# A two-layer gated cross-attention and FFN kernel: the first FFN's weights turned and split inside the attention's last slots, and the butterfly's path products moved to the FFN's first stage

## What is computed

```python
x = x + tanh(g_xattn[0]) * L0_attention(layernorm(x), ctx)     # 16 heads of 16
# first FFN, quantised
x1 = act_qdq(layernorm(x))              # one scale for the whole tensor
up = act_qdq(x1 @ lpbq_dequant(w_up).T)     # w_*: 4 bit, blocks of 32, 768 x 256
gate = act_qdq(x1 @ lpbq_dequant(w_gate).T)
sig = fixed_qdq_u16(sigmoid(gate))
gate = act_qdq(gate * sig)
x = x + tanh(g_ffn[0]) * (act_qdq(gate * up) @ lpbq_dequant(w_down).T)
x = x + tanh(g_xattn[1]) * L1_attention(layernorm(x), ctx)     # 8 heads of 64
# second FFN: W_exp, 10 butterfly stages of width 1024, gelu, 10 stages, W_con
x = x + tanh(g_ffn[1]) * L1_ffn(layernorm(x))
```

## Time and profile before

| | |
|---|---|
| median of three runs | 1106.67 us |
| the profiled execution: its own time, its span | 1109.04, 1106.8 us |
| mean granted TensorE clock | 0.917 |
| busy in the span: PE, DVE, ACT, POOL | 937.6, 788.3, 616.5, 247.8 us |
| setup and slots of the first attention | 0 to 302 us |
| first FFN: setup block, to the first gate product | 302 to 323 us |
| gate products; up products; code stage; down products | 323 to 399; to 487; to 552; to about 650 us |

### The profile page before, as it was taken

How to read it: one execution, slowest core, us unless ns; L and a number is a source line. 1 busy time by engine, 2 the same in 40 slices (tenths; PEclk the granted TensorE clock), 3 DMA queues, 4 the chain that set the end, 5 groups by cost and what they waited for, 6 DMA issues and landing times. The chain is left out here.

```text
span 1106.8 us, 20169 instructions
## 1 busy us (share of the span) xinstructions
PE 937.6 (85%) x6641; PEld 830.2 (75%) x6641; DVE 788.3 (71%) x1585; ACT 616.5 (56%) x1067; POOL 247.8 (22%) x436
## 2 busy tenths in 40 slices
PE   6589999999569998824088994999999998999998
PEld 5467787877358876613088993999999986999888
DVE  5358888874339989879979833677777777766671
ACT  4147777764367779968747633556656653322230
POOL 4223333320139200013004202111111104111210
PEclk9779999997769999966579996999999998999999
DMA  6755555552042237778422367755656620000001
GB/s 189 219 132 143 143 142 142 145 172 81 6 159 115 114 119 235 254 254 288 147 79 73 138 205 169 171 122 121 124 124 125 125 65 1 20 20 26 31 19 39
DMA packets 101076, 138.31 MB, mean 125 GB/s; under 512 B 42758, under 2 KB 76550, under 8 KB 98582
## 3 DMA queue, kind: packets, MB, share of 16 engines
q1 hardware_dynamic: 100102, 135.23, 43.3%
q10 hardware_dynamic: 608, 1.18, 0.5%
q0 software_dynamic: 304, 1.10, 0.3%
HBM read 71.04 MB, written 47.13 MB: 107 GB/s over the span
## 5 line engine op out<-in xcount | busy, mean ns | idle before, releaser
L2645 ACT ACTIVATE f_h<-bank,f_b 128x512 f32<-128x512 f32 x64 | 43.4, 691 | 112.1 <-PE bank L43 64.3
L665 DVE TENSOR_REDUCE a_maxima<-bank 128x4 f32<-128x308 f32 x128 | 60.4, 472 | 43.8 <-PE bank L738 42.5
L41 PE MATMUL bank<-f_xt_hi,f_w_all 128*128 128x512 f32 x192 | 77.5, 404 | 11.9 <-DMA f_xt_lo<-x_spill 9.9
L599 ACT ACTIVATE a_prob<-bank 77x512 f32<-77x512 f32 x128 | 72.2, 588 | 19.5 <-PE bank L763 19.2
L42 PE MATMUL bank<-f_xt_lo,f_w_all 128*128 128x512 f32 x192 | 75.8, 395 | 0.0
L43 PE MATMUL bank<-f_xt_hi,f_w_all 128*128 128x512 f32 x192 | 75.7, 394 | 0.0
L760 PE MATMUL bank<-a_stack,a_kb 96*77 96x256 f32 x256 | 72.5, 306 | 1.1 <-ACT a_prob L599 0.6
L43 PE MATMUL bank<-f_w_hi,f_h_lo 128*128 128x256 f32 x256 | 72.2, 282 | 0.0
L42 PE MATMUL bank<-f_w_lo,f_h_hi 128*128 128x256 f32 x256 | 72.2, 282 | 0.0
L41 PE MATMUL bank<-f_w_hi,f_h_hi 128*128 128x256 f32 x256 | 72.0, 281 | 0.0
L763 PE MATMUL bank<-a_mt,a_pick 128*77 128x256 f32 x256 | 67.9, 288 | 0.0
(11 more groups left out here) (322 smaller groups left out, 3173.8 us busy)
## 6 DMA issues: line engine op xcount, KB each, us to landing
u_spill<-f_ubuf SPq DMA_DIRECT2D x48, 256.0 KB, 2.7
f_w_all<-u_spill SPq DMA_DIRECT2D x24, 512.0 KB, 4.4
a_stack<-a_queries SPq DMA_DIRECT2D x16, 512.0 KB, 5.2
a_q_max<-a_q_hi SPq DMA_DIRECT2D x30, 256.0 KB, 4.9
a_kb<-a_key_spill SPq DMA_DIRECT2D x96, 77.0 KB, 2.5
xres<-in_x SPq DMA_DIRECT2D x16, 256.0 KB, 4.6
a_queries<-a_q_hi SPq DMA_DIRECT2D x16, 256.0 KB, 3.8
a_queries<-a_q_lo SPq DMA_DIRECT2D x16, 256.0 KB, 4.1
```

The lines of the kernel that those rows point to most:

```text
L41: nc.tensor.matmul(out, w_hi, m_hi, start=start, stop=False)
L599: act.activation(prob[0:S, n % 4, :, :].rearrange("p a b -> p (a b)"), (S0, S1)[n % 2][0:S, :], ACT.Exp, scale=SCALE).then_inc(probs, 1)
L665: dve.tensor_reduce(maxima[:, t, 4 * k:4 * k + 4], MX[:, 0:4 * SE].rearrange("p (h s) -> p h s", s=SE)[:, :, 0:S], AX.X, ALU.max).then_inc ...
L2645: act.activation(h[:, n % 2, :], hbank[n % 4][:, :], ACT.Gelu, bias=b1[:, n:n + 1]).then_inc(h_ready, 1)
```

## The change

- The split weights of the first FFN (`w_all`, `d_hi`, `d_lo`) are allocated before the attention (`FirstFfn`). While the attention's setup runs, they hold the context's and the projections' split parts; the weights to be quantised (`fw`) lie where the keys were, so their loads wait for the keys' store.
- The store to `w_quantised`, the load of it and the whole setup block of the FFN go away. In slots 13, 14 and 15 three steps are added, `turn0` to `turn2`: four transposes on TensorE into bank T0, a 128x512 copy on ScalarE and a 128x512 subtraction on VectorE each, nine in all. The scale of x and the gate's tanh move to the start of the FFN's first block. There VectorE encodes and casts half of the first group.
- The butterfly's low paths are read in one DMA (128x4064) at the head of that block, ahead of the gate's value `tg`, into the room of the `hid` tile that the last two groups fill later. GpSimd forms the path products ahead of the top stages; SyncE stores them (`blocks_spill`) and they are read back in the code stage, behind chunk 5; `y` is read behind chunk 7 and `z` behind chunk 9.
- The three early reads of `u_spill` stand behind all 48 stores.
- In the code stage ScalarE codes all 24 chunks of up. The five units of `y` and the bias stand behind chunks 19 to 23. The four units of `z` move to the next stage: TensorE makes them behind the maximum's spread, ahead of the down products, and ScalarE copies two of them out before each of its first two splits.

```diff
         wo_lo = sb("wo_lo", [P, C, D], F32R)
-        k_hi = sb("k_hi", [P, B, C, SE], F32R)
-        k_lo = sb("k_lo", [P, B, C, SE], F32R)
+        keys_then_fw = sb("keys_then_fw", [P, 2 * B * C * SE])
+        k_hi, k_lo = (keys_then_fw[:, n * B * C * SE:(n + 1) * B * C * SE].bitcast(F32R).rearrange(
+            "p (b c s) -> p b c s", c=C, s=SE) for n in range(2))
...
+        PE_SLOT = "s0 s1 xt turn0 mx0 s2 t3 s3 mx1 s4 q0 turn1 mx2 p1 s5 mx3 p3 s6 mx4 s7 at0 mx5 t0 q1 turn2 mx6 p5 t1 mx7 pr0 pr1 mt t2 p7".split()
+        ACT_SLOT = "s0 s1 xt turn0 s2 st2 s3 p1 s4 turn1 s5 p3 s6 at0 q1 turn2 s7 xn p5 mt p7".split()
+        DVE_SLOT = "mx0 xs turn0 mx1 norm mx2 w0 w1 w2 turn1 mx3 ln mx4 w3 mx5 as mx6 am w4 turn2 mx7 qs pu st1 w5".split()
...
-        SP_SLOT = "xl qw vb k0 qr k1 fw".split()
+        SP_SLOT = "xl qw vb k0 qr k1".split()
...
         def _(sp):
+            sp.wait_ge(kb_stored, 32)
             for n, w in enumerate(("w_gate", "w_up")):
...
-                elif what == "fw":
-                    sp.wait_ge(fw_done, FW_PIECES)
-                    for n in range(3):
-                        sp.dma_start(ffn["quantised"][:, n, :], fw[:, n * FW:(n + 1) * FW]).then_inc(fw_sent, 16)
-
             slots(sp, SP_SLOT, step, SP_SLOT)
-            sp.wait_ge(fw_sent, 48)
...
+                elif what[:4] == "turn":
+                    n = (b - FW_FROM) * 3 + int(what[4])
+                    act.wait_ge(fw_turned, n + 1)
+                    act.activation(FW_TURNS[n][1][0], T0[:, :], ACT.Copy).then_inc(fw_rounded, 1)
...
+                elif what[:4] == "turn":
+                    n = (b - FW_FROM) * 3 + int(what[4])
+                    dve.wait_ge(fw_rounded, n + 1)
+                    dve.tensor_tensor(FW_TURNS[n][1][1], T0[:, :], FW_TURNS[n][1][0].bitcast(F32),
+                                      ALU.subtract).then_inc(fw_split, 1)
...
+                elif what[:4] == "turn":
+                    n = (b - FW_FROM) * 3 + int(what[4])
+                    if n == 0:
+                        pe.wait_ge(fw_done, FW_PIECES)
+                        pe.wait_ge(q_split, B)
+                    else:
+                        pe.wait_ge(fw_split, n)
+                    for k, (tile, col) in enumerate(FW_TURNS[n][0]):
+                        at = tile * D + col
+                        last = pe.transpose(T0[:, k * P:(k + 1) * P], fw[:, at:at + P], ident[:])
+                    last.then_inc(fw_turned, 1)
...
-            @block.sync
-            def _(sp):
-                for n in range(3):
-                    sp.dma_start(wval[:, n * FT:(n + 1) * FT, :].rearrange("p f d -> p (f d)"),
-                                 weights[:, n, :]).then_inc(w_in[n], 16)
-                sp.dma_start(tg[:], gate).then_inc(g_in, 16)
...
-            @block.tensor
-            def _(pe):
...
-                    last.then_inc(turned, 1)
...
                 dve.tensor_scalar(x_step[:], env["rstd_all"][:], codes[:, SX:SX + 1], None, ALU.mult).then_inc(x_scaled, 1)
                 dve.tensor_scalar(x_start[:], env["nmr_all"][:], codes[:, SX:SX + 1], None, ALU.mult).then_inc(x_scaled, 1)
+                dve.wait_ge(x_scaled, 2)
+                for t in range(GTT // 2, GTT):
+                    last = dve.tensor_scalar(xcode[:, t, :], xres[:, t, :], x_step[:, t:t + 1], x_start[:, t:t + 1],
+                                             ALU.mult, ALU.add)
+                last.then_inc(x_half, 1)
+                dve.wait_ge(x_half, 1)
+                dve.tensor_copy(xn[:, GTT // 2:GTT, :], xcode[:, GTT // 2:GTT, :]).then_inc(x_half, 1)
...
+                act.wait_ge(g_in, 16)
+                act.activation(tg[:], tg[:], ACT.Tanh)
                 act.wait_ge(x_scaled, 2)
-                encode(0)
-                cast(0)
+                encode(0, GTT // 2)
+                cast(0, GTT // 2)
+                act.wait_ge(x_half, 2)
                 encode(1)
...
+                        if g == PATH_GROUP and f == 0:
+                            act.wait_ge(blocks_stored, 16)
...
+                pool.wait_ge(paths_in, 16)
+                for s in range(1, LOW):
+                    for net in range(2):
...
+                sp.dma_start(paths, bf["low_paths"]).then_inc(paths_in, 16)
+                sp.dma_start(tg[:], gate).then_inc(g_in, 16)
                 for g in range(G - 2):
+                    if g == PATH_GROUP - 2:
+                        for net in range(2):
+                            sp.wait_ge(composed[net], LOW - 1)
+                        sp.dma_start(bf["blocks_dram"], paths[:, 2 * LOWEST:2 * LOWEST + 2 * HT * P]).then_inc(
+                            blocks_stored, 16)
...
-                    if k == PREFETCH_AT and f == FT - 1:
-
-                        sp.wait_ge(prods, GATES)
-                        for i in range(NR):
-                            written = ORDER.index(i * CW // (2 * FT * T)) * FT + FT
-                            for n in range(NU):
-                                sp.wait_ge(u_sent[n], 16 * ((written + NU - 1 - n) // NU))
-                            fetch_up(sp, i)
+                for i in range(NR):
+                    written = ORDER.index(i * CW // (2 * FT * T)) * FT + FT
+                    for n in range(NU):
+                        sp.wait_ge(u_sent[n], 16 * ((written + NU - 1 - n) // NU))
+                    fetch_up(sp, i)
...
-            DVE_CODES = [1, 9, 17]
...
+            UNITS_FROM = NCH - HT // 2 - 1
+            DVE_CODES = []
...
-                sp.dma_start(blocks[:].rearrange("p n t m -> p (n t m)"), bf["low_last"]).then_inc(last_in, 16)
                 for n in range(len(u_sent)):
                     sp.wait_ge(u_sent[n], 16 * GATES // len(u_sent))
-                sp.dma_start(early[:], bf["low_early"]).then_inc(early_in, 16)
                 for i in range(NR, NCH):
                     u_in(i)
                     if i == 5:
+                        sp.dma_start(blocks[:].rearrange("p n t m -> p (n t m)"), bf["blocks_dram"]).then_inc(blocks_in, 16)
+                    if i == 7:
                         sp.dma_start(y[:], bf["w_exp_t"].rearrange("(t p) d -> p t d", p=P)).then_inc(y_in, 16)
-                    if i == 7:
+                    if i == 9:
                         sp.dma_start(z[:], bf["w2_dram"]).then_inc(z_in, 16)
...
-                pe.wait_ge(composed[0], LOW - 1)
+                pe.wait_ge(blocks_in, 16)
                 pe.wait_ge(y_in, 16)
-                for n in range(HT // 2 + 1):
-                    unit(n)
-                pe.wait_ge(composed[1], LOW - 1)
-                pe.wait_ge(z_in, 16)
-                for n in range(HT // 2 + 1, len(UNITS)):
-                    unit(n)
+                pe.wait_ge(multiplied, UNITS_FROM - 1)
+                for n in range(HT // 2):
+                    for t in range(2 * n, 2 * n + 2):
+                        last = pe.matmul(unit_bank[n][:, (t - 2 * n) * D:(t - 2 * n + 1) * D], blocks[:, 0, t, :],
+                                         y[:, t, 0:D], start=True, stop=True)
+                    last.then_inc(unit_prod, 1)
...
-                for b in range(4):
-                    hi(b)
+                for n in range(HT // 2):
+                    act.wait_ge(unit_prod, n + 1)
+                    act.activation(z[:, 2 * n:2 * n + 2, :], kv_banks[n][:, :].rearrange("p (t d) -> p t d", d=D),
+                                   ACT.Copy).then_inc(unit_out, 1)
+                    if n % 2:
+                        hi(n // 2)
+                hi(2)
+                hi(3)
...
+                pe.wait_ge(z_in, 16)
+                for n in range(HT // 2):
+                    if n == HT // 2 - 1:
+                        pe.wait_ge(e_scale, 1)
+                    for t in range(2 * n, 2 * n + 2):
+                        last = pe.matmul(kv_banks[n][:, (t - 2 * n) * D:(t - 2 * n + 1) * D], blocks[:, 1, t, :],
+                                         z[:, t, :], start=True, stop=True)
+                    last.then_inc(unit_prod, 1)
```

234 lines of the change are left out of this document (102 added, 132 removed).

## The result

The changed kernel takes **1096.96 us**, the median of 5 runs (1093.79 to 1100.34); the kernel before takes 1106.67 us (5 runs, 1104.99 to 1108.11). The ratio is 0.9914, with a 95% interval of 0.9888 to 0.9940. Forecast were 1090.8 us and a range of 1084 to 1100. The profiled execution took 1098.77 us, with a span of 1097.0 us and a mean granted clock of 0.919.

The account below looks back on a forecast made before the run. The prediction took the kernel as a chain of stages, where gains at five hand-overs reach the end unless the clock takes them back. Terms -3.8 - 5.6 - 1.3 - 4.2 - 1.0 = -15.9 off 1106.67 gave 1090.8 us, range 1084 to 1100.

Parts of the forecast that it names:

- Term 1: Attention slots 13 to 15: added turns cost 0.6, 0.6 and 1.2 us, slot 14 at full clock saves 6.2; -3.8 us.
- Rival 1: Slot 14 of the attention: the clock falls all the same, slots 13 to 15 become +2.0 us, total 1096.6 us; chance 0.28.
- Term 2: Start of the first FFN: weight reload and transposes gone, `tg` waits behind the paths; first gate product -5.6 us, bounds -4.3 to -12.8.
- Term 3: End of the up products: three early reads no longer stand ahead of the last six stores; -1.3 us.
- Term 4: Code stage: path products moved out, VectorE codes no chunk and sets the pace; 58.1 us against 62.3, -4.2 us.
- bound by the reads: Code stage: 1 MB reads behind chunks 5, 7 and 9 set the pace, its saving falls to nothing, 1095 us; chance 0.08.
- Term 5: Start of the down products: first split 1.4 us later, twenty-nine products at full clock save 2.7; together -1.0 us.

## Why the prediction was right, and for which reasons it was not

The direction and the range were right: 9.7 us were gained and 15.9 forecast. That the time fell inside the range was in part luck: one term had the wrong sign, one most of its size missing, and a gain that no term had looked at made up for much of both.

**Term 1 failed at the step "If it stays at full, slot 14 is like slot 13, with 19.35 - 13.12 = 6.2 us less. I take that."** The fall of the clock in slot 14 was read from one execution and charged to every one. In its second profile the kernel before, with a wait of 1.34 us in the same place, ran slot 14 in 13.84 us, and the three profiles with other addresses had 13.52, 13.57 and 13.62. Against those 38.03 us for the three slots the change has 38.9: where the clock doesn't fall, term 1 is +0.9, not -3.8. Against the mean of the two profiles, 40.9, it is -2.0; how often the timed runs of the kernel before had the fall, no run shows. The wait for keys did go, as forecast, but not by the reason given: it stays away with the store put back too. The added turns were priced about right: slot 13 is 0.60 longer than in the first profile (0.6 forecast), slot 15 is 0.39 longer (1.2 forecast). The prediction's own sentence that its durations come from an execution 2.4 us above the median should have been a warning: the fall alone made it some 5.5 us longer (19.35 against 13.84).

**Rival 1**, that the clock falls all the same, gives 1096.6, and the time came out at 1097.0; but not by its mechanism. The clock stayed full through slots 13 to 15 with the transposes in them, in all nine profiles of kernels that have the turns. The rule of the Trainium skill behind it (TensorE: Matmul & The Clock Gate, Part 4: PE-mode transpose: a transpose doesn't count as busy in the same way) is neither borne out nor refuted by that, since four transposes stand among score products; against it still speak. That 1096.6 is so near is luck.

**Term 2 held, at its nearer bound**: -4.6 measured from the scale to the first product in the first profiles and -3.9 in the second ones (18.66 to 14.75), -4.3 on the mean; -5.6 was forecast, with a bound of -4.3. The mechanism, `tg` behind the paths, was right to the row. What was off in the first profile is the landing: 9.9 us instead of 9.3, from an issue 0.4 us later than I had it. With `tg` first, the price of the wait is 8.0 us; I had given 7.2 for it.

**Term 3**: the idle time of 1.65 and 1.31 us at the last up products is gone, as forecast. But gate and up products together took 167.2 us before and 166.9 after, on the mean of two. After the change the first gate products run at 1.2 GHz for 6.2 and 3.7 us, before it for 2.9 and 5.4, and the stage is longer the longer that lasts; at equal length the change is, by an estimate from the fourteen profiles, some 0.5 us shorter. So it is -0.2 by the means and perhaps -0.5, instead of -1.3.

**Term 4 failed at "The 1 MB reads between the chunk reads may starve ScalarE at `y`, whose rows are short: 0.6".** Most of the rest was right: VectorE's multiplications all take 1.21 to 1.23, none is stretched, and the kernel with the reads cut has the stage at 58.09 us, where 58.1 were forecast. But whole reads cost 3.1 us more than that and not 0.6 in all: each of 1 MB makes ScalarE wait once or twice, and VectorE, which lost its own extra work with the change, now waits with it. The waits stood in the profile of the kernel before (3.9 us), and the prediction didn't read them. VectorE idle in the code stage was one of its own signs of being wrong. This is most of the rival "bound by the reads", to which I gave 0.08. Term 4 is -1.2 on the mean, of -4.2.

**Term 5 held**: -0.7 on the mean of two, -1.0 forecast. The first down product is 1.55 us later (+1.4 forecast), and the clock is full when it comes.

**What was missing**: the eleven slots ahead of the change, -4.0 on the mean (151.98 to 148.02). No part of the prediction looked at what the removed DRAM tensor stood in front of. Nor does that explain all of it: with the old addresses 2.7 of the 4.0 us stay, and their cause is open.

Sum of these: -4.0 + 0.9 - 4.3 - 0.2 - 1.2 - 0.7 = -9.5, against -9.7 between the medians. The agreement is closer than the evidence. The sum leaves out the first profile's fall in slot 14 (-2.9 on the mean of two), the start (-1.7), the down stage and the way behind it (+0.4, +0.9) and the slot near the end (+2.3); with them it is the -10.5 between the mean spans. Term 1 by itself missed by 4.7 us and term 4 by 3.0; the eleven slots gave 4.0 back.

The best kernels of the study are the change with `tg` first and the reads cut, 1086.15 us, and the same with the earlier split, 1085.27. By the ratios to the kernel before they are 12 and 10 us faster than the change, and nothing tells them apart.

## What to carry to other kernels

A clock that falls once in a profiled execution need not be a cost of every execution: profile the same kernel twice before a term of several microseconds is built on it, and look whether the gap ahead of the fall is there without the fall. A large transfer on the queue of a prefetch cost a wait wherever it stood, because the read behind it landed later than its lead; in pieces of a quarter it cost next to nothing. Waits that cost nothing before can cost their full length once the engine behind them gets faster, so read them in the profile of the kernel before. A median over a window that cuts a repeating pattern at another place isn't the same figure: compare the same reads. And a small transfer that someone waits for goes ahead of the large one: here two swapped lines gave 8.7 us on top of the 9.7 of the whole change.

## What the runs showed of the hardware that was not expected

- The same reads of queries, 512 KB each, landed in 5.2 us with the spill declared at one place in DRAM and in 4.7 to 4.8 us with it 1.31 MB lower, and TensorE's waits for keys in eleven slots fell from 5.0 to 0.5 and 0.8 us. Nothing else in the program differed. The Trainium skill (DMA: Bandwidth & Descriptors, Latency and other measured facts) ties the rate of copies between tensors in HBM to the pitch of their rows, at large powers of two; here no pitch was changed, only where the tensor begins. Why the place matters is open, and no gain in the timed runs is shown.
- One kernel, one place: behind a gap of 2.42 us the clock fell to 1.2 GHz in the first profile of the kernel after, behind 2.41 us it stayed at 2.4 GHz in the second. In the kernel before it fell behind 2.43 us and stayed behind 2.46.
- Half a kilobyte took 2.0 us to land ahead of 2 MB and 9.9 us behind them on its queue, with 1 MB beside it on POOL's queue, which took 9.9 us where it had taken 6.0.
